# One-core graph network kernel: rows of source terms by DMA in the third layer alone, TensorE broadcasts in all graphs elsewhere

## What is computed

```python
# layer 0: attention with 4 heads of 32, masked by adj
q, k, v = x @ wq.T + bq, x @ wk.T + bk, x @ wv.T + bv
out = softmax(where(adj == 0, -inf, q k.T / sqrt(32))) @ v ; out @ wo.T + bo
# layer 1: h = x @ W; e = leaky_relu(s1[:, None] + s2[None, :], 0.2), masked; softmax(e) @ h
# layer 2: the same with 8 heads of 16, plus a constant log prior; then @ W_out.T
# layer 3: relu(x @ w1 + b1), an UNMASKED attention of width 256 ("l3"), elu(elu(.)) + residual,
#          relu(. @ w2 + b2), a masked attention of width 128 ("l3b"), elu(elu(.)) + residual, relu
```

## Time and profile before

| what | value |
|---|---|
| median of 3 executions | 1070.28 us (1068.1 to 1076.06) |
| the profiled execution | 1069.56 us |
| its span in the profile | 1067.7 us |
| TensorE busy | 999.2 us (94%) |
| VectorE busy | 910.9 us (85%) |
| ScalarE busy | 763.6 us (72%) |
| GpSimd busy | 403.2 us (38%) |

### The profile page before, as it was taken

How to read it: one execution, slowest core, us unless ns; L and a number is a source line. 1 busy time by engine, 2 the same in 40 slices (tenths; PEclk the granted TensorE clock), 3 DMA queues, 4 the chain that set the end, 5 groups by cost and what they waited for, 6 DMA issues and landing times. The chain is left out here.

```text
span 1067.7 us, 25731 instructions
## 1 busy us (share of the span) xinstructions
PE 999.2 (94%) x8649; PEld 731.7 (69%) x8649; DVE 910.9 (85%) x2499; ACT 763.6 (72%) x2022; POOL 403.2 (38%) x660
## 2 busy tenths in 40 slices
PE   7999999999999999999999999999999999998995
PEld 4776666775667677676868677776867576856774
DVE  3988998889899798998899999788889996899654
ACT  4789875785888687788877789797866836544653
POOL 1013333250444562434736371653535272320111
PEclk9999999999999999999999999999999999999998
DMA  4001111021212120312203130310202120320000
GB/s 128 2 22 43 60 64 60 21 91 45 68 44 70 52 87 27 102 42 75 73 27 93 41 113 11 92 41 32 82 26 87 32 82 1 101 70 22 11 10 21
DMA packets 41530, 57.89 MB, mean 54 GB/s; under 512 B 12728, under 2 KB 15288, under 8 KB 41400
## 3 DMA queue, kind: packets, MB, share of 16 engines
q1 hardware_dynamic: 40536, 55.98, 17.2%
q10 hardware_dynamic: 864, 0.26, 0.1%
HBM read 51.12 MB, written 5.11 MB: 53 GB/s over the span
## 5 line engine op out<-in xcount | busy, mean ns | idle before, releaser
L1329 DVE SCALAR_TENSOR_TENSOR P<-row,t2e,mask_t 128x512 f32<-128x512 f32 x512 | 367.4, 776 | 13.3 <-PE bank L689 10.9
L856 ACT ACTIVATE probs<-probs,low 128x512 f32<-128x512 f32 x256 | 185.6, 727 | 46.4 <-DVE low L1128 45.5
L1128 DVE CUSTOM_DVE_ANT_0 probs<-bank,mask_add 128x512 f32<-128x512 f32 x256 | 170.1, 675 | 10.2 <-PE bank L582 10.1
L867 ACT ACTIVATE probs_t<-bank 128x512 f32<-128x512 f32 x232 | 136.3, 606 | 19.8 <-PE bank L590 19.4
L590 PE MATMUL bank<-ident,probs 128*128 128x128 f32 x1024 | 139.6, 277 | 7.0 <-ACT probs L856 5.5
L590 PEld LDWEIGHTS bank<-ident,probs 128*128 128x128 f32 x1024 | 112.8, 141 | 44.4 <-ACT probs L856 25.1
L902 ACT ACTIVATE x<-x,shift_l,rstd_l 128x128 f32<-128x128 f32 x256 | 105.3, 487 | 47.9 <-POOL shift_l L1486 47.5
L1471 POOL TENSOR_TENSOR rstd_l<-mv_l,ln_eps 128x4 f32<-128x4 f32 x64 | 19.8, 309 | 303.8 <-DVE mv_l L1197 303.8
L734 PE MATMUL bank<-t,l_P 128*128 128x258 f32 x512 | 119.3, 387 | 4.9 <-DVE low L1128 2.1
L689 PE MATMUL bank<-P,GH 128*32 128x512 f32 x1024 | 118.2, 602 | 4.5 <-issue 2.3
L734 PEld LDWEIGHTS bank<-t,l_P 128*128 128x128 f32 x512 | 95.9, 192 | 20.9 <-DVE low L1128 2.3
(11 more groups left out here) (179 smaller groups left out, 1958.3 us busy)
## 6 DMA issues: line engine op xcount, KB each, us to landing
row<-l_line SPq DMA_DIRECT2D x158, 256.0 KB, 3.8
x_in<-in_x SPq DMA_DIRECT2D x16, 256.0 KB, 2.6
out<-x SPq DMA_DIRECT2D x15, 256.0 KB, 2.0
row<-l3b_line SPq DMA_DIRECT2D x10, 256.0 KB, 3.0
l_P<-in_adj SPq DMA_DIRECT2D x4, 256.0 KB, 4.5
l_line<-turned SPq DMA_DIRECT2D x26, 16.0 KB
l_line<-l_turned SPq DMA_DIRECT2D x20, 16.0 KB
w_fc<-in_L_gnn_W_fc SPq DMA_DIRECT2D x1, 256.0 KB, 3.8
```

Of the source, the lines that this page charges most:

```text
L856: act.activation(e, e, ACT.Exp, bias=low0[:, m:m + 1], scale=-1.0, accum_out=g.of(den0)[:, m:m + 1])\
L867: act.activation(probs_t[c % 2][:, h, :, :].rearrange("p j n -> p (j n)"), ps("l0_t", g, m)[:, :], ACT.Copy)\
L1128: dve.tensor_tensor_reduce(probs[c % 2][:, h, :], ps("l0_s", g, m)[:, :], mask_add[:, c, :], 1.0, LOWEST, ALU.add, ALU.min, low0[:, m:m + ...
L1329: last = dve.scalar_tensor_tensor(P2[:, h % GROUP2, j, :], row("l2_spread", g, h)[:, :], g.of(t2e)[:, j, h:h + 1], mask_t[:, j, :], ALU.ma ...
```

## The change

`ROWS_BY_DMA` and all that hangs on it goes: in all sixteen graphs l1, l3, l3b get their rows and l0 its reciprocals by TensorE, and VectorE does `l0_o` and `l3_p`. Layer 2 keeps its DMA rows, now with five row buffers in turn. The reciprocals are no longer laid out by head. GpSimd clears no padding tiles at the start. The loads of wq, wk, wv come first and have `proj_in` for themselves; bq and bk have a semaphore that ScalarE waits for, bv one that VectorE waits for in graph 0. `SPLIT_TURNED` (the copies by VectorE in graphs 0 to 2) and `IN_HALVES` (the halves at the end) stay. The orders of the engines and the banks are written anew.

By the order strings: `l0_rd`, `l1_s`, `l3_s`, `l3b_s` stand 16 times each and not 6; `warm` 58 times and not 65 (eight fewer between the opening and graph 12's part, one more in the opening); GpSimd's `l3_p` 0 and not 40, its `l0_o` 0 and not 10; VectorE's `l3_p` 64 and not 24, its `l0_o` 16 and not 6, its turns for l0, l1, l3 and l3b 0 and not 40; SyncE has 80 stages fewer; 1334 bank uses and not 1294. ScalarE's stages are the same in another order.

```diff
-ROWS = 6
+ROWS = 5
-ROWS_BY_DMA = range(2, 12)
 ...
-        for name, n in [("proj_in", 6 * 16), ("out_in", 3 * 16), ...
+        for name, n in [("proj_in", 3 * 16), ("bias_qk_in", 2 * 16), ("bias_v_in", 16), ("out_in", 3 * 16), ...
 ...
+        def row(g, h):
+            return rows[(HEADS2 * g.i + h) % ROWS]
 ...
+            def l2_spread(g, h):
+                if h == 0:
+                    sp.wait_ge(*sig("l2_rows", g, 16))
+                if HEADS2 * g.i + h >= ROWS:
+                    sp.wait_ge(signal["p2_made"], HEADS2 * g.i + h - ROWS + 1)
+                sp.dma_start(row(g, h)[:, :], g.of(line2)[h * C:(h + 1) * C, :].rearrange("c p -> (c p)")
+                             .rearrange("(o n) -> o n", o=1).broadcast_to([P, N_NODES])).then_inc(row_done(g, h)[0], 16)
 ...
             def l0_y(g, k):
-                pe.wait_ge(*divided(g))
+                pe.wait_ge(*took("l0_rd", g))
 ...
             def l3_o(g, c):
                 if c == 0:
-                    pe.wait_ge(*sources_read("l3", g))
+                    pe.wait_ge(*took("l3_s", g))
 ...
-                "mask_T": mask_T, "proj_T": turn_raw("proj_T", ("wq", "wk", "wv"), "proj_in", 6 * 16),
+                "mask_T": mask_T, "proj_T": turn_raw("proj_T", ("wq", "wk", "wv"), "proj_in", 3 * 16),
 ...
             def proj_load(g, k):
-                loaded = signal["proj_in"]
-                for n, key in (("wq", "L0_gnn_wq"), ("wk", "L0_gnn_wk")):
-                    act.dma_start(rawf[:, RAW[n] * D:(RAW[n] + 1) * D], w[key]).then_inc(loaded, 16)
-                act.dma_start(bias_q[:, 0:1], w["L0_gnn_bq"].rearrange("(p o) -> p o", o=1)).then_inc(loaded, 16)
-                act.dma_start(bias_k[:, :], w["L0_gnn_bk"].rearrange("(p o) -> p o", o=1)).then_inc(loaded, 16)
-                act.dma_start(rawf[:, RAW["wv"] * D:(RAW["wv"] + 1) * D], w["L0_gnn_wv"]).then_inc(loaded, 16)
-                act.dma_start(bias_v[:, :], everywhere(w["L0_gnn_bv"], D)).then_inc(loaded, 16)
+                for n, key in (("wq", "L0_gnn_wq"), ("wk", "L0_gnn_wk"), ("wv", "L0_gnn_wv")):
+                    act.dma_start(rawf[:, RAW[n] * D:(RAW[n] + 1) * D], w[key]).then_inc(signal["proj_in"], 16)
+                act.dma_start(bias_q[:, 0:1], w["L0_gnn_bq"].rearrange("(p o) -> p o", o=1)).then_inc(signal["bias_qk_in"], 16)
+                act.dma_start(bias_k[:, :], w["L0_gnn_bk"].rearrange("(p o) -> p o", o=1)).then_inc(signal["bias_qk_in"], 16)
+                act.dma_start(bias_v[:, :], everywhere(w["L0_gnn_bv"], D)).then_inc(signal["bias_v_in"], 16)
 ...
             def l0_rcp(g, k):
                 dve.wait_ge(*sig("den0_safe", g, 1))
                 if g.has(1):
-                    dve.wait_ge(*(dma_sig("l0_turned", g, 1, back=1) if by_dma(g, 1) else wrote("l0_rd", g, back=1)))
+                    dve.wait_ge(*wrote("l0_rd", g, back=1))
 ...
-                        dve.wait_ge(*(spread_done(n + "_spread", g) if by_dma(g) else wrote(n + "_s", g)))
+                        dve.wait_ge(*wrote(n + "_s", g))
                         if g.has(1):
                             dve.wait_ge(*wrote(n + "_o", g, 1, back=1))
-                    made = dve.scalar_tensor_tensor(q["P"][:, j, :], sources(n, g), q["b"][:, j:j + 1],
+                    made = dve.scalar_tensor_tensor(q["P"][:, j, :], ps(n + "_s", g)[:, :], q["b"][:, j:j + 1],
                                                     mask_t[:, j, :], ALU.max, ALU.mult)
 ...
-            def l0_o(g, k):
-                pool.wait_ge(*spread_done("l0_spread", g))
-                for c in range(C):
-                    pool.wait_ge(*took("l0_pv", g, c))
-                pool.wait_ge(*wrote("l0_y", g, back=1))
-                pool.tensor_tensor(o0_t[:, :], row("l0_spread", g)[:, :], o0_raw[:, :], ALU.mult).then_inc(signal["o0_made"], 1)
-
-            def l3_p(g, j):
-                q = gat["l3"]
-                if j == 0:
-                    pool.wait_ge(*sig("l3_b", g, 3))
-                    pool.wait_ge(*spread_done("l3_spread", g))
-                    pool.wait_ge(*wrote("l3_o", g, C - 1, back=1))
-                made = pool.tensor_scalar(q["P"][:, j, :], row("l3_spread", g)[:, :], q["g"][:, j:j + 1], q["b"][:, j:j + 1],
-                                          ALU.mult, ALU.max)
```

More of the change, by code:

```diff
@@ L212, in bank_uses @@
     return used
-def row_uses():
-    used, transfers, last, at = {}, [0] * ROWS, [None] * ROWS, 0
-    for name, g, k in turns("sp"):
-        if name.endswith("_spread"):
-            r = int(ROW_OF_USE[at])
-            at += 1
-            transfers[r] += 1
-            used[name, k, g.i] = r, transfers[r], last[r]
-            last[r] = name, k, g
-    return used
 def build_program(nc, x, adj, w, out):
     use = bank_uses()
-    row_use = row_uses()
     with ExitStack() as ctx:
@@ L344, in build_program @@
         for n in GATS:
-            for what, k in (("c4", 1), ("dd", 2), ("b", 3), ("turned", 1), ("p", 1)):
+            for what, k in (("c4", 1), ("dd", 2), ("b", 3)):
                 sem(f"{n}_{what}", k)
@@ L388, in empty, with row_done @@
             return bank[b]
-        def by_dma(g, back=0):
-            return g.i - back in ROWS_BY_DMA
-        def dma_sig(name, g, k=1, back=0):
-            return signal[name], per_graph[name] * ROWS_BY_DMA.index(g.i - back) + k
-        def sources_read(n, g, back=0):
-            return dma_sig(n + "_p", g, 1, back) if by_dma(g, back) else took(n + "_s", g, 0, back)
-        def divided(g, back=0):
-            return dma_sig("o0_made", g, 1, back) if by_dma(g, back) else took("l0_rd", g, 0, back)
-        def row(stage, g, k=0):
-            return rows[row_use[stage, k, g.i][0]]
-        def spread_done(stage, g, k=0):
-            r, transfers, _ = row_use[stage, k, g.i]
-            return row_filled[r], 16 * transfers
-        def row_read(stage, g, k):
-            if stage == "l2_spread":
-                return sig("p2_made", g, k + 1)
-            return divided(g) if stage == "l0_spread" else sources_read(stage[:-len("_spread")], g)
-        line = {n: [nc.dram_tensor(f"{n}_line{q}", [BLOCK, P], F32, kind="Internal").ap() for q in range(2)]
-                for n in ("l0", "l1", "l2", "l3", "l3b")}
+        def row(g, h):
+            return rows[(HEADS2 * g.i + h) % ROWS]
+        def row_done(g, h):
+            n = HEADS2 * g.i + h
+            return row_filled[n % ROWS], 16 * (n // ROWS + 1)
+        line2 = [nc.dram_tensor(f"line2_{q}", [HEADS2 * C, P], F32, kind="Internal").ap() for q in range(2)]
         x_v = x.rearrange("b (p c) d -> b p c d", c=C)
@@ L872, in l0_ov @@
                 if g.has(1):
-                    act.wait_ge(*divided(g, back=1))
+                    act.wait_ge(*took("l0_rd", g, back=1))
                 act.activation(o0_raw[:, c * P:(c + 1) * P], ps("l0_pv", g, c)[:, 0:P], ACT.Copy)\
@@ L1316, in l2_cap, with l2_turn @@
                     .then_inc(signal["small2_made"], 1)
+            def l2_turn(g, k):
+                dve.wait_ge(*sig("exp2", g, 1))
+                if g.has(1):
+                    dve.wait_ge(*sig("l2_rows", g, 16, back=1))
+                dve.transpose(turned2[:, :], g.of(R2)[:, :]).then_inc(signal["l2_turned"], 1)
             def l2_p(g, h):
-                dve.wait_ge(*spread_done("l2_spread", g, h))
+                dve.wait_ge(*row_done(g, h))
                 if h == 0:
@@ L1425, in _ @@
                 "l3_c4": column_max("l3", t3, "l3_h", 4), "l3_dmax": max_target("l3"), "l3_dd": scores("l3", t3),
-                "l3_p": l3_p, "l3_rcp": l3_rcp, "l3_z": l3_z, "l3_zT": l3_zT,
+                "l3_p": weights("l3", 3), "l3_rcp": l3_rcp, "l3_z": l3_z, "l3_zT": l3_zT,
                 "l3b_c4": column_max("l3b", t4, "l3_h2", 2), "l3b_dmax": max_target("l3b"),
```

316 lines of the change are left out of this document (130 added, 186 removed), and 11 rows, old and new, of the table STAGES.

## The result

The changed kernel takes 1059.59 us (median of four, 1058.64 to 1062.58) against 1070.32 us for the kernel before (median of four, 1068.1 to 1076.06). The ratio is 0.9896, 95% interval 0.987 to 0.9922: **faster by 1.0%**, where I had forecast slower by 1.6%. The profiled execution took 1058.64 us, its span is 1056.8 us.

A forecast was written before the change was run, and what follows sets the result against it. The prediction took TensorE to bound the middle, with VectorE close behind. Its terms 22.7 - 4 + 2 - 3 = +17.7 us on the profiled 1069.56 us gave 1087 us, range 1068 to 1100 us.

The forecast's parts named there:

- What bounds the kernel: Middle, 100 to 930 us: TensorE, busy 95.5%, is the bound, with VectorE close behind at 89.4%.
- The remaining 37 us of the middle: TensorE's idle time from 100 to 930 us, where it is busy for 792.5 of 830 us.
- rival (a): Middle: slack takes the added work, TensorE's share rises to 97.7%, time 1067 us, not slower; chance 0.17.
- the order as a whole packs better: All engines: caveat that the new order may pack better or worse by more than the added work; no size given.
- no change of the clock: Middle: granted clock 0.99, the upper of two levels (2.4 GHz), expected to stay.
- Part 1: TensorE, graphs 2 to 11: l1_s, l3_s, l3b_s, l0_rd add 22.7 us; eight fewer filler turns, taken as -4.
- Part 2: l3_p and l0_o from GpSimd to VectorE: net +24 us on VectorE, bounds +12 and +29, beside TensorE's added work.
- Rival (b): VectorE and the banks bind, 1099 us; sign: VectorE share above about 93% in the middle; chance 0.20.
- Part 3: Old waits for GpSimd go, new waits for banks and l0_rd come: net +2 us, bounds -3 and +10.
- Part 4: DMA queue: 80 transfers fewer, five row buffers instead of six; priced at 0, else VectorE waits before l2_p.
- Part 5: Opening: wv loads third and only matrices are waited for, transposes start earlier; -3 us, bounds -3.5 and 0.
- (c): l2_p's stretching all goes with GpSimd's work, and half of TensorE's 37 us idle goes: 1058 us; chance 0.07.

The follow-up runs named there:

- a_less_pe: Kernel after with two of four matmuls left out of every second part of l3_o in graphs 2 to 11 (-17.4 us of TensorE): 1057.91 us.
- b_less_pe: Kernel before with the same two of four matmuls left out of every second part of l3_o in graphs 2 to 11: 1070.08 us, ratio 0.9988.
- b_pe_rows: Kernel before, its orders otherwise held, with rows of l0, l1, l3, l3b by TensorE and l0_o, l3_p on VectorE, old loads: 1105.3 us, ratio 1.0321.
- a_old_loads: Kernel after with the opening's loads as they were before (one semaphore, wv fifth): 1062.28 us, ratio 0.9923.
- b_l3_rows: Kernel before with only l3's rows by TensorE and forty l3_p moved from GpSimd to VectorE in graphs 2 to 11: 1091.65 us, ratio 1.0217.
- b_short_pool: Kernel before with GpSimd's l3_p on 64 of 512 columns, orders unchanged: 1060.93 us, ratio 0.9914.

## Why the prediction was wrong

**What bounds the kernel: the step that failed.** I read TensorE's 95.5% as the bound, and paid its added work in full. a_less_pe and b_less_pe show that it wasn't: 17 us less give next to nothing in either kernel. The remaining 37 us of the middle were not a fixed tax on such an order either: the new order, with shorter chains between exponential and weights, left 22.7 of 820 us. That they were handovers between engines that wait for each other in a fixed order is what is left when neither TensorE's work nor VectorE's, taken away, gives its time back; it wasn't measured handover by handover. The prediction's own rows had said as much: stretches of 49.1 and 49.6 in 50, which I listed for rival (a) and gave 0.17. I had also written that the forecast is wrong above all if the order as a whole packs better; it had no chance of its own in the sum, so it stood at nothing, and it was the largest term: some 43 us between b_pe_rows and a_old_loads, against 17.7 for everything that I had priced. I also expected no change of the clock; it rose from 0.991 to 0.995.

**Part 1, TensorE's added work.** Right in size: l0_rd's pitch is 0.98 us again (341.79 to 342.77 in the trace after), and from the first matmul of each added stage to the first of the group behind it the forty stages sum to about 25 us, for the 22.7 forecast: the median of a stage of four transposes is 0.49 us, and the 0.43 of the earlier trace rows was one of the shorter ones. Fillers: busy time down by 5.3 us (35.9 to 30.6), forecast 4.4. Wrong in effect: TensorE's busy time rose by 6.5 us, where I had forecast some 20; other groups are listed with less than before (L734, l3_o, 119.3 us before and 116.7 after; L689, l2_v, 118.2 and 116.5).

**Part 2, VectorE.** Right in size: 64 l3_p of 794 ns (forecast 800), l2_p's mean 763 ns (765), l2_p's longest 1284 ns for 3755. Busy time rose by 14.3, not by 24. I put it beside TensorE's work, at no price of its own. With the order held that is the worst miss: b_l3_rows alone costs 23.7 us. Rival (b), VectorE and the banks, at 1099 us, is close to b_pe_rows at 1105, and a part of its mechanism is there (l0_s behind a bank that l_P holds, 5.1 us). Its other sign, a VectorE share above 93% in the middle, is not: b_pe_rows has 732.2 of 830 us, 88%. So it is near the truth for the order of before, in part by luck, and the change didn't keep that order.

**Part 3, the waits.** Forecast +2. The new waits are small where the order was drawn for them (4.5 us of VectorE in all) and large where it wasn't. **Part 4, the row buffers.** Right: VectorE waits 0.2 us in all for rows of l2. **Part 5, the opening.** Forecast -3, measured -2.7 and -3.3.

**The rivals.** The time lies below (a), 1067 us, whose mechanism is the nearest: TensorE's share rose to 97.2%, as it asked for (97.7%). (c) named the time, 1058 us, by luck. Its sum has a slip: half of the 37 us is 18.5 and not 9, which would have made 1048. And its reason failed: it wanted the stretching of l2_p to go, and its mean fell by only 13 ns, 7 us in all. The l2_p of 3755 ns that spoke for it stands beside other work of GpSimd than the work that left, though it was gone in b_short_pool too. The part of it that holds is that GpSimd's results were waited for: b_short_pool gives 8.7 us for less of GpSimd's work, with 6.6 us less of VectorE's time in it.

**What stays open.** The 43 us belong to the new order and the new route together. The order of before leaves a median of 9.0 us from exponential to weights, the new one 3.4. Whether an order for the old route, drawn with the same care, would have gained as much was not tried, and so it isn't shown how the 43 us divide between shorter chains and better packing. Nor is it shown how much of them are the places that I gave VectorE's forty l3_p in the held order.

## What to carry to other kernels

A busy share of 95% is not yet a bound: take 2% of the work of that engine away, and if the time stays, its work isn't what is paid for. Look at the granted clock of those runs too, since it can hide a part of the gain. When a change rewrites the order, do the same edit in the old order first; the order's part is then a measured number (here some 43 us, beside 18 us of priced work), as good as the places given to the moved work. In this kernel less work on GpSimd gained time though it was busy for only a third of the span, and work moved onto VectorE cost its full time until the order was drawn for it.

## What the runs showed of the hardware

Forty GpSimd instructions of 128x512 whose results nobody reads cost 20 us, and left the 512 instructions of VectorE's l2_p at a median of 745 ns (747 without them), while they themselves took 2072 to 3737 ns. Beside GpSimd's 128x128 instructions with two SBUF inputs l2_p has a median of 883 ns in the kernel after, and 747 beside none. TensorE's clock fell to its lower level for 3.4 us after idle stretches of 1.5 to 2.1 us, and over 82 runs of one kernel 0.001 of mean clock goes with about 1 us. The long l2_p of 3755 ns of the kernel before was gone in b_short_pool as well (the longest there is 1762 ns). A row took 17.6 us from exponential to weights in the long case shown with the DMA queue, 1.9 us in the short one with TensorE. In the held order it took 5.7 to 22.4 us with TensorE too. Of the 17.6, VectorE took 2.8 to come to the turn, and SyncE's issues of seven reads, of l2's rows too, stretch from 391.72 over 13.19 us; how long the row had lain ready before VectorE used it the rows don't say.
